# Sixteen small tiles for the conditioning product, and where its low parts are made

## The reference, cut to what matters

```python
W = weights[condition]                       # (128, 32, 32), one of 16 matrices per batch
h = einsum('bct,bcd->bdt', x, W)             # mixing: 32 x 32 per batch, over 512 positions
q_c = h @ Wq_c.T + bq_c                      # 512 -> 192
kv  = h @ Wkv_c.T + bkv_c                    # 512 -> 128
...
x = x + attention(h);  x = x + ffn(conv(x))
```

## Time and profile before

| | |
|---|---|
| median of 3 runs | 771.8 us |
| profiled execution: span from first to last instruction | 770.2 us |
| what lies around the span (median less span) | 1.6 us |
| TensorE busy | 753.3 us, 98% |
| VectorE busy | 620.6 us, 81% |
| ScalarE busy | 379.9 us, 49% |
| GpSimd busy | 200.2 us, 26% |
| TensorE clock granted | 1.000 over the span |

### The profile page before, as it was taken

How to read it: one execution, slowest core, us unless ns; L and a number is a source line. 1 busy time by engine, 2 the same in 40 slices (tenths; PEclk the granted TensorE clock), 3 DMA queues, 4 the chain that set the end, 5 groups by cost and what they waited for, 6 DMA issues and landing times.

```text
span 770.2 us, 18485 instructions
## 1 busy us (share of the span) xinstructions
PE 753.3 (98%) x7769; PEld 598.4 (78%) x7769; DVE 620.6 (81%) x1109; ACT 379.9 (49%) x675; POOL 200.2 (26%) x203
## 2 busy tenths in 40 slices
PE   9999999999999999999999999999999799999996
PEld 7777686778668777868786786778677699999996
DVE  5676899989998796777769776878889688888887
ACT  2575546546563774655465546545655322222221
POOL 5002020020002010270200000000040688888872
PEclk9999999999999999999999999999999999999999
DMA  9910010020001000001200010002207158889861
GB/s 231 237 58 5 3 59 2 1 60 2 2 2 59 2 1 29 1 4 23 77 1 2 2 56 2 1 2 59 84 2 193 63 139 205 204 206 204 204 134 69
DMA packets 42738, 51.74 MB, mean 67 GB/s; under 512 B 7024, under 2 KB 29600, under 8 KB 42656
## 3 DMA queue, kind: packets, MB, share of 16 engines
q1 hardware_dynamic: 40384, 49.87, 25.5%
q0 software_dynamic: 1056, 0.49, 0.3%
q10 hardware_dynamic: 1216, 0.19, 0.2%
HBM read 41.91 MB, written 8.63 MB: 66 GB/s over the span
## 4 chain that ended last, share of the span: by engine, by line
PE 91%; DVE 6%; ACT 1%; issue 1%; POOL 0%; DVEq 0%
PE ps L730 33%; PE ps L598 9%; PE ps L599 8%; PE ps L600 8%; PE ps L774 6%; PE ps L797 4%; PE ps L1084 4%; PE ps L616 4%; PE ps L1085 4%; PE ps L1053 2%; PE ps L693 1%; PE ps L1041 1%; PE ps L1043 1%; PE ps L1042 1%; PE ps L1067 1%
## 5 line engine op out<-in xcount | busy, mean ns | idle before, releaser
L1185 ACT ACTIVATE qt<-ps,m_bias 128x512 f32<-128x512 f32 x228 | 145.8, 686 | 100.2 <-PE ps L730 100.2
L730 PE MATMUL ps<-q_high,m_high 64*128 64x512 f32 x768 | 154.4, 397 | 0.5 <-issue 0.5
L730 PE MATMUL ps<-q_high,m_low 64*128 64x512 f32 x768 | 150.6, 387 | 0.0
L730 PE MATMUL ps<-q_low,m_high 64*128 64x512 f32 x768 | 108.3, 386 | 0.0
L1445 DVE TENSOR_TENSOR z_low<-ps,z_high 128x512 fp32r<-128x512 f32 x128 | 79.6, 681 | 14.4 <-ACT z_high L1203 12.9
L730 PEld LDWEIGHTS ps<-q_high,m_high 64*128 64x128 f32 x768 | 72.4, 184 | 22.3 <-issue 7.9
L528 POOL TENSOR_TENSOR o_sum<-o_part,o_part 128x512 f32<-128x512 f32 x7 | 9.1, 1301 | 290.6 <-ACT o_part L1213 290.6
L730 PEld LDWEIGHTS ps<-q_low,m_high 64*128 64x128 f32 x768 | 72.5, 184 | 14.9
L730 PEld LDWEIGHTS ps<-q_high,m_low 64*128 64x128 f32 x768 | 72.5, 184 | 13.8
L1203 ACT CAST z_high<-ps 128x512 fp32r<-128x512 f32 x128 | 66.7, 597 | 13.1 <-PE ps L797 8.9
L1190 ACT ACTIVATE sc<-sc 128x512 f32<-128x512 f32 x60 | 37.7, 633 | 48.4 <-DVE sc L1430 48.4
(11 more groups left out here) (294 smaller groups left out, 1652.1 us busy)
## 6 DMA issues: line engine op xcount, KB each, us to landing
x_in<-in_x SPq DMA_DIRECT2D x16, 512.0 KB, 4.2
x_s<-in_x SPq DMA_DIRECT2D x32, 256.0 KB, 5.3
out<-res SPq DMA_DIRECT2D x31, 256.0 KB, 3.4
toep_high<-taps_scratch SPq DMA_DIRECT2D x32, 192.0 KB, 4.2
toep_low<-taps_scratch SPq DMA_DIRECT2D x32, 192.0 KB, 4.7
toep_far<-taps_scratch SPq DMA_DIRECT2D x32, 64.0 KB, 5.1
wq_nope<-in_L_attn_Wq_up SPq DMA_DIRECT2D x2, 768.0 KB, 10.1
wq_nope<-in_L_attn_Wq_up SPq DMA_DIRECT2D x1, 1536.0 KB, 17.5
```

The costliest lines, as they stand in the source:

```text
L730: mm = pe.matmul(ps[:, fold_bank(u, j) + e, :], weights[rows, (GH * g + j) // 2, c, :], moving[c][rows, :], start=start, stop=stop)
L1185: act.activation(qt[:, j, :], ps[:, fold_bank(u, j) + j % 2, :], ACT.Identity, bias=m_bias[:, h:h + 1]).then_inc(s["qt_done"], 1)
```

## The change

- From the second group on, each gathered 32x32 matrix is itself the stationary operand. For each of four sets of four batches (n), four column tiles (j, a quarter of the positions within each 128) and four row tiles (b, the batch) make 16 matmuls of 32 rows x 32 columns x 128 moving columns: 64 for a group, one bank of PSUM for each b. One wait ahead of all: the seventh low part of the values and the second `take_scores`.
- The result has the mixed channel on partitions. VectorE turns its 32x32 blocks from PSUM into `h_raw` in SBUF (four 128x512 transposes, after all 64 matmuls). ScalarE casts `h_high` from `h_raw`, and GpSimd subtracts for `h_low` (four 128x512, SBUF only), and then gathers the next group's weights. GpSimd's spreading of weights (L479) is gone; group 0 keeps the old mixing, with weights spread by VectorE.
- TensorE: output quarters 1, 2 and 3 come before the projections. Of projections ca and ab the products with `h_high` come first (16), then those with `h_low` (4 for ca, 4 for ab), then kv. This order holds for group 0 also.
- ScalarE: `soft(0)`, `soft(1)`, `soft(2)` all ahead of `projected_ca` and `projected_ab`. VectorE: the transposes come ahead of the first angle steps; `below_max(2)` ahead of `projected_ca`; `projected_ab` ahead of the last angle steps.

```diff
+            def mixed_low(k):                      # GpSimd
+                for b in range(4):
+                    pool.wait_ge(s["h_high_done"], 4 * k + b + 1)
+                    pool.tensor_tensor(batch_h(h_low, b), batch_raw(b), f(batch_h(h_high, b)),
+                                       ALU.subtract).then_inc(s["h_low_done"], 1)
+                if k + 1 < NS:
+                    gather(2 * k + 2)
+                    gather(2 * k + 3)
...
+            def mixed_x(k):                        # TensorE
+                pe.wait_ge(s["zl_done"], 8 * (2 * k - 2) + 7)
+                pe.wait_ge(s["s_taken"], 4 * (2 * k - 1) + 2)
+                for n in range(4):
+                    i, g = 2 * k + n // 2, n % 2
...
+                    for j in range(4):
+                        for b in range(4):
+                            rows, to = slice(32 * b, 32 * b + 32), slice(32 * j, 32 * j + 32)
+                            mm = pe.matmul(ps[to, MIX_BANK[b], :].rearrange("e (s n q) -> e n s q", s=TT, n=4)[:, n],
+                                           gathered[i % 2][rows, g, :],
+                                           x_in[i % 2][rows, g, :].rearrange("c (s j q) -> c j s q", s=TT, j=4)[:, j],
+                                           start=True, stop=True)
+                    mm.then_inc(s["h_ready"], 1)
...
+            def project(k):
+                if k == 0:
+                    pe.wait_ge(s["wcT_done"], 2)
+                pe.wait_ge(s["h_high_done"], 4 * k + 4)
+                project_high(1, BZ + 1)
+                if k >= 1:
+                    pe.wait_ge(s["s_taken"], 4 * (2 * k - 1) + 3)
+                project_high(0, BX)
+                pe.wait_ge(s["h_low_done"], 4 * k + 4)
+                project_low(1, BZ + 1).then_inc(s["qca_ready"], 1)
+                project_low(0, BX).then_inc(s["q_ready"], 1)
...
-                    mixed_x(i)
-                    mixed_x(i + 1)
+                    mixed_x(i // 2)
                     output(u - 1, 1)
                     output(u - 1, 2)
-                    project_ca(i // 2)
-                    project_ab(i // 2)
+                    output(u - 1, 3)
+                    project(i // 2)
                     project_kv(i // 2)
-                    output(u - 1, 3)
...
+            def mixed_high(k):                     # ScalarE
+                for b in range(4):
+                    act.wait_ge(s["h_turned"], 4 * (k - 1) + b + 1)
+                    act.copy(batch_h(h_high, b), batch_raw(b)).then_inc(s["h_high_done"], 1)
...
-                    mixed_high(i)
-                    mixed_high(i + 1)
-                    soft(u, 0)
-                    soft(u, 1)
+                    mixed_high(i // 2)
+                    for n in range(3):
+                        soft(u, n)
                     projected_ca(i // 2)
-                    soft(u, 2)
                     projected_ab(i // 2)
                     projected_kv(i // 2)
...
+            def mixed_turned(k):                   # VectorE
+                dve.wait_ge(s["h_ready"], 4 * k + 4)
+                for b in range(4):
+                    dve.transpose(h_raw[:, b, :], ps[:, MIX_BANK[b], :]).then_inc(s["h_turned"], 1)
...
+                    mixed_turned(i // 2)
+                    below_max(u, 0)
                     angles(turn[0], turn[1])
-                    mixed_low(i)
-                    mixed_low(i + 1)
-                    below_max(u, 0)
+                    below_max(u, 1)
                     angles(turn[1], turn[2])
-                    below_max(u, 1)
+                    below_max(u, 2)
                     projected_ca(i // 2)
-                    below_max(u, 2)
+                    projected_ab(i // 2)
                     angles(turn[2], turn[3])
-                    projected_ab(i // 2)
                     below_max(u, 3)
```

More of the change, by code:

```diff
@@ L168, in build @@
     x_in = [t(f"x_in{n}", [P, 2, T], at=at) for n, at in enumerate((x_at, h_at + 4 * KB))]
-    h_high = t("h_high", [P, 2, TT, HT], F32R, at=qt_at + 16 * KB)
-    h_low = t("h_low", [P, 2, TT, HT], F32R, at=qt_at + 24 * KB)
+    h_high = t("h_high", [P, TT, ST], F32R, at=qt_at + 16 * KB)
+    h_low = t("h_low", [P, TT, ST], F32R, at=qt_at + 24 * KB)
+    h_raw = t("h_raw", [P, 4, ST], at=ph_at)
     q_high, q_low = ([t(f"q_{part}{n}", [P, ST], F32R, at=(q_at + (2 * k + n) * 2 * KB if n < 2 else h_at + 2 * k * KB))
@@ L302, in build @@
     TURN_BANK = (BS,) + (BZ,) * (QUADS - 1)
-    MIX_BANK = lambda i, e: (BS + e if i % 2 else BT + e if i == 0 else (BT + 1, BZ)[e])
+    FIRST_MIX_BANK = lambda i, e: BS + e if i else BT + e
+    MIX_BANK = (BT + 1, BZ, BS, BS + 1)
     TAP_BANK = (BZ, BX)
@@ L325, in x_arrived, with first_h, batch_h, batch_raw @@
         return s[("x_loaded", "x1_loaded")[i % 2]], 16 * (i // 2 + 1)
-    def mix_of(i):
-        return mix if i % 2 == 0 else mix_first if i == 1 else mix_odd
+    def first_h(tile, i, n):
+        return tile[:, 2 * n:2 * n + 2, i * HT:(i + 1) * HT]
+    def batch_h(tile, b):
+        return tile[:].rearrange("p s (n b e) -> p b (s n) e", n=4, b=4)[:, b]
+    def batch_raw(b):
+        return h_raw[:, b, :].rearrange("p (a e) -> p a e", e=C)
     x_v = d["x"].rearrange("(g b) c t -> (b c) g t", b=4)
@@ L543, in decayed @@
                 chain(pool.tensor_tensor(g_t[:, hs, :], g_t[:, hs, :], tu[:, :, 0, :], ALU.add))
[L545 to L548, removed]
+            for u in range(1, LAST):
+                if u % 2 == 0:
                     summed(u // 2 - 1)
[L551 to L561, removed]
+                elif u == 7:
+                    pool.wait_ge(s["turn_sin"], 4)
+                    decay(0)
+                    mixed_low(4)
+                    for n in range(3):
+                        decayed(n)
+                        decay(n + 1)
+                    decayed(3)
+                    pool.sem_inc(s["gf_ready"], 1)
+                else:
+                    mixed_low((u + 1) // 2)
             pool.wait_ge(s["t_ready"], GH * LAST)
@@ L600, in three, with first_x @@
                 return pe.matmul(out, ll, rh, start=False, stop=stop)
-            def mixed_x(i):
+            def first_x(i):
                 pe.wait_ge(*x_arrived(i))
                 pe.wait_ge(s["mix_ready"], i + 1)
[L605 to L609, removed]
+                if i == 1:
                     pe.wait_ge(s["wcT_done"], 2)
@@ new lines, in project_high, with project_low @@
+            def project_high(m_, bank):
+                for tt in range(TT):
+                    pe.matmul(ps[:, bank, :], wcT_high[:, tt, m_, :], h_high[:, tt, :], start=(tt == 0), stop=False)
+                    pe.matmul(ps[:, bank, :], wcT_low[:, tt, m_, :], h_high[:, tt, :], start=False, stop=False)
+            def project_low(m_, bank):
+                for tt in range(TT):
+                    mm = pe.matmul(ps[:, bank, :], wcT_high[:, tt, m_, :], h_low[:, tt, :], start=False, stop=(tt == TT - 1))
+                return mm
@@ L640, in project_kv @@
                     pe.wait_ge(s["wcT_done"], 3)
[L641 to L644, removed]
+                project_high(2, BZ)
+                project_low(2, BZ).then_inc(s["kv_ready"], 1)
             def turn_latent(k):
@@ L1518, in first_weights @@
             def first_weights(i):
-                tile = mix_of(i)
+                tile = (mix, mix_first)[i]
                 dve.wait_ge(s["first_mix"], 2 * i + 2)
```

62 lines of the change are left out of this document (20 added, 42 removed).

## The result

The change made the kernel slower by 1%: 780.5 us (median of 9 runs, 773.8 to 783.4) against 772.0 before, ratio 1.0099 with a 95% interval of 1.0081 to 1.0118. I had forecast 772.3 in a range of 762 to 780: the measured time stands at its upper edge (the ratio, applied to the 771.8 from which I had started, gives 779.4).

What follows compares the result with a forecast made beforehand. TensorE was taken as the bound (91% of the chain, full clock). Span 770.2 - 12.6 + 0.5 + 8.5 + 3.4 + 0.7 = 770.7, plus 1.6 from span to median: 772.3 us, range 762 to 780.

Steps and rivals of the forecast that it cites:

- The mixing: The 64-matmul block in seven groups: 1.7 us in place of 3.49, -12.6 us; unit 1's wait at its start, +0.5.
- Rival C: In the mixing, the 16 tiles don't run side by side: 3.5 us, nothing saved, stalls stay, 785 us; chance 0.06.
- `h_high`: From mixing to h_high: transposes and ScalarE's casts done at T + 3.4, needed at T + 4.1; cost nothing.
- T: Start of the output quarter behind the mixing, from which the prediction counts its times in us.
- `h_low`: GpSimd's four subtractions, slowed by turns with VectorE: ready 0.2 us before needed at T + 7.7; cost nothing.
- turns: VectorE and GpSimd operations with both sources in SBUF don't run beside each other: 1.70 us for a pair.
- Rival B: h_low becomes TensorE's wait in every group, +1.3 us in seven groups, partly instead of fold stalls: 779 us; chance 0.17.
- The return to the fold: TensorE waits for ab's high part at the next fold: 3.1 us from units 1 and 5, 2.3 from unit 3; +8.5.
- Rival A: The turns don't happen as counted; the folds cost 0.8 us and the units behind about 2.6: 764 us; chance 0.30.
- The units behind: VectorE's lateness reaches the value blocks: +1.9 us in unit 2, +1.5 in unit 4, sum +3.4, bounds 0 and 5.
- The start: Group 0 gets the new order: ab's high part 0.5 us later, first product waits 0.2 for the casts; +0.7.

Runs made afterwards that it cites:

- padded kernel after: The changed kernel with 48 one-column matmuls (192 TensorE instructions) more at the start, behind the warm-up; 807.2 us, ratio 1.041.

## Why the prediction came out as it did

The direction was left open (0.44 for slower), the size was 8 us short. By its steps:

1. *The mixing.* 1.83 us, and 0.09 for the entry from another tile form: 1.92 in place of the 1.7 that had both changes of form in it. Seven blocks save 11.0, not 12.6. That was the right row to go by, with the size 13% off. Rival C is refuted. Unit 1's wait is 0.4 (0.5). The rule of the Trainium skill (TensorE: Matmul & The Clock Gate, Part 3, "Measured speedup vs the span model"), by which I had estimated near 17, does not hold here: the block took 1.83 us, not near 1.0.
2. *`h_high`.* T + 3.3 against T + 3.4; no wait in any group.
3. *`h_low`.* T + 7.5 as worked out, with turns of the predicted lengths, and no wait in any group. Rival B is refuted, though by 0.4 us.
4. *The return to the fold.* Places, releaser and chain as predicted: `below_max(2)` at T + 12.6 (12.5), ab's high part at T + 15.2 (15.1), stalls 2.7, 1.9, 2.7 (3.1, 2.3, 3.1), none for units 8 to 14. Rival A is refuted by 7.3 us of stalls. The run without the subtractions is 8.0 us faster in the medians, and I had put 8.3 between A and the forecast, but that is partly luck: between the two profiled executions it is 11.8, the stalls 7.5, the clock 2.6, the fetch stalls 2.1 and the start 0.5, less 0.9 for longer waits at the value blocks. **What I left out here is what stands behind the stalls**: in the profiled execution the clock fell behind two of them, +2.6. I had read the full clock of the earlier trace rows as a property of the kernel; it was that of a TensorE which never stood for more than 1.4 us from unit 1 to the end of attention. The fall is not certain: in one of the two executions with SP's later loads the gaps of 2.66 and 2.73 us are followed by 0.68 and 0.67 over 4 us and folds 1.6 us longer, in the other the same gaps are followed by 1.00 twice.
5. *The units behind.* 0.7 and 1.6 more than before (1.9 and 1.5 predicted). In the profiled execution unit 2's fold ran 1.3 us longer at the lower clock, which gave VectorE that much time; in the second execution with SP's later loads, at full clock, the wait is 1.93 us.
6. *The start.* 1.9 against 0.7. Of it 1.3 stands ahead of the first moved instruction: the mixing of group 0's second half starts at 14.74 here, at 13.75 to 14.54 in the four other profiled executions with this start, and at 13.47 before. From there to `products(2)` it is 15.8 us in all five and 15.2 before: the step itself is 0.6.

**The step that failed is the sum itself**: it took all that lies outside the six steps, above all behind unit 14, as moved and not changed. 1344 more instructions of TensorE shifted the boundaries of its fetches, one of them fell into the densest block of the last stages while SP filled the DMA queues, and TensorE stood for 5.4 us (+6.0 with the clock, +1.1 in unit 11). In the medians, SP's later loads take 4.5 us from the changed kernel (780.5 and 776.05, of two sets of runs) and 1.3 from the kernel before. The last value blocks have that stall in every profiled kernel with the changed instruction list and SP's old loads (5.4, 5.3 and 3.9 us). The kernel before had a row of the same kind, 1.32 us of "issue" at 598, which I did not look at since it was small and far from the change. The difference, 3.2, makes 775.5 of the 772.3. The other 5.0 of the median are the mixing with its entries (1.6), the ways to the next fold (0.7), unit 11 (1.1), some of the clock's 2.6 and a start that is 0.3 to 1.3 later, less the smaller stalls and value blocks (some 2). These terms are of single executions, and the sum can't be made closer by them: the runs of the changed kernel spread over 9.7 us, those before over 2.3.

What stays open: why a fetch begins as late as it does. All 13 profiled executions together have 22 "issue" gaps of 0.7 us or more from unit 1 to the end of attention. In 21 of them TensorE went on 1.2 to 1.5 us behind the end of a fetch, which had begun between 1.6 us ahead of the stop and 2.8 behind it (the exception is a gap of 0.92 in the padded kernel after). That the gaps are waits for instructions is read from this; what holds a fetch back beside SP's traffic no run shows. Nor do the runs show whether all seven groups could pay, with the angle steps moved out of units 1 to 5: that wasn't tried.

## What to carry to other kernels

Before giving work to GpSimd, look at what VectorE does at that moment: operations of both with two sources in SBUF take turns, and where VectorE's list is the later one the turns reach TensorE; put the work in units where VectorE has slack (with SP's loads held, four groups of small tiles took 2.6 us off, where all seven added 5.0). A change that adds instructions moves every fetch boundary behind it, so look for "issue" gaps of TensorE in dense small-tile blocks, above all beside bulk loads, and hold those loads back if their data are not yet needed. A long stall is priced with the slower clock that may stand behind it (2.7 us cost up to 4.3 here).

## What the runs showed of the hardware

- Sixteen 32x32 tiles with 128 moving columns: 128 records of plain float32 in 1.83 us, 14.3 ns a record, against 11.9 for 32x64 tiles with 64 columns.
- About 256 instructions of TensorE come in one fetch. A block that uses them up in 1.6 to 1.8 us can outrun it: gaps of 0.7 to 1.7 us inside mixings, 2.0 in the last value block. The DMA engines need not be busy for it: during the gaps of 1.71 in a mixing (padded kernel after, 549 us) and 2.01 in the last value block (SP's loads held) their share is 0.00.
- The granted clock after a stall is not settled by its length: from unit 1 to the end of attention, in all profiled executions, it stayed full behind every gap of 1.2 to 1.94 us (16 of them), fell in part or all of the next 2 us behind 8 of 15 gaps of 1.99 to 2.73 us, the same place falling in one execution and not in the next, and behind all four of 3.9 to 5.4 us.
- Matmuls of one moving column are dear. At full clock a record of theirs took 0.11 us to the next, as much as one of the old mixing with 128 columns (0.109), and 0.21 at half of it. The clock fell among them, though they ran back to back (granted 1.00 from 7.35 to 9.5 us, 0.53 from 9.5 to 12), and was 0.50 from 12 to 20 us, where it is full without them:

```profile
7.35 4.72 PE L923 MATMUL ps<-busy 128*128 128x1 f32 x32
```
```profile
12.00:20.00 8.00, 8.00 (x40) 8.00 (x39) 1.29 (x6) 1.76 (x3) 2.05 (x3) 0.50 1.07 252
```
